# The residual held as upper and lower halves of images: 48 loads of whole images for 160 pieces, one store per piece for two

## The reference, cut to what matters

```python
x = x + conv(_ln_c(x), ...)        # an involution: 7x7 filters that depend on the position
t = to_tokens(x)                   # 16 * 3136 = 50176 tokens of 64 channels
t = t + ffn(_ln_t(t), ...)         # 8 experts, each token goes to its best 2
x = from_tokens(t, x)              # back to images x channels x positions
```

## Time and profile before

| | |
|---|---|
| time, median of 3 runs | 2610.99 us (2604.84 to 2629.76) |
| the profiled execution's own time | 2621.96 us |
| its span, first to last instruction | 2619.3 us |
| mean granted TensorE clock | 0.874 |
| TensorE busy | 2025.6 us (77%) |
| VectorE busy | 1506.3 us (58%) |
| ScalarE busy | 829.4 us (32%) |
| GpSimd busy | 961.0 us (37%) |
| moved by DMA | 474.16 MB, mean 181 GB/s |

### The profile page before, as it was taken

One profiled execution on the slowest core, in us unless ns is written; L12 is line 12 of the kernel. 1 busy time (PEld: TensorE's weight loads), 2 busy tenths in 40 slices (PEclk: granted clock), 3 DMA queues, 4 the chain that ended last, 5 costly groups with the idle time before them and its releaser, 6 DMA issues. The chain is left out here.

```text
span 2619.3 us, 34529 instructions
## 1 busy us (share of the span) xinstructions
PE 2025.6 (77%) x10208; PEld 1223.9 (47%) x10208; DVE 1506.3 (58%) x2687; ACT 829.4 (32%) x1540; POOL 961.0 (37%) x1011
## 2 busy tenths in 40 slices
PE   8959889898898998899898321477778777787855
PEld 5735444454444455445454321345455445454534
DVE  4536666566778777786787535245444444444434
ACT  3421111122222222222222211355445454554520
POOL 6110000004242142331343566155555555555540
PEclk9969999999899999899999555689898898988976
DMA  9877777778776777777773311666667666676539
GB/s 278 176 149 193 184 178 186 196 196 195 181 198 171 203 196 194 182 193 183 195 207 90 89 55 46 174 192 194 187 200 196 194 187 196 195 195 190 164 104 356
DMA packets 284717, 474.16 MB, mean 181 GB/s; under 512 B 116144, under 2 KB 188387, under 8 KB 261565
## 3 DMA queue, kind: packets, MB, share of 16 engines
q1 hardware_dynamic: 247965, 423.23, 60.5%
q0 software_dynamic: 30528, 34.27, 4.8%
q10 hardware_dynamic: 6048, 14.57, 1.5%
HBM read 392.67 MB, written 81.93 MB: 181 GB/s over the span
## 5 line engine op out<-in xcount | busy, mean ns | idle before, releaser
L967 POOL DMA_INDIRECT token_rows<-gate_rows,gate_index x392 | 408.3, 1042 | 1043.4 <-DVE gate_index L1289 930.8
L1167 DVE TENSOR_TENSOR prod<-z_ps,r_all 119x896 f32<-119x896 f32 x512 | 544.8, 1084 | 221.5 <-PE z_ps L1080 110.2
L1500 POOL DMA_INDIRECT mixed<-exp_mix,exp_xt x474 | 491.0, 1036 | 409.8 <-DVE exp_mix L1639 282.7
L1523 ACT ACTIVATE exp_hid<-exp_h_ps,exp_pack 128x384 f32<-128x384 f32 x632 | 349.1, 575 | 419.3 <-PE exp_h_ps L1567 192.8
L1084 PE MATMUL z_ps<-xq,band 112*119 112x448 f32 x1024 | 440.2, 565 | 44.3 <-DVE prod L1167 38.4
L1567 PE MATMUL exp_h_ps<-exp_tok,exp_pack 128*128 128x384 f32 x1264 | 293.0, 377 | 61.7 <-issue 61.2
L1084 PEld LDWEIGHTS z_ps<-xq,band 112*119 112x119 f32 x1024 | 182.1, 187 | 254.8 <-issue 190.7
L1567 PEld LDWEIGHTS exp_h_ps<-exp_tok,exp_pack 128*128 128x128 f32 x1264 | 237.1, 208 | 79.9 <-issue 74.2
L1097 PE MATMUL o_ps<-prod,pick 119*32 119x448 f32 x2048 | 247.9, 578 | 26.9 <-issue 17.2
L1579 PE MATMUL exp_y_ps<-exp_hid,exp_pack 128*64 128x384 f32 x1264 | 262.4, 540 | 1.1 <-issue 1.1
L1078 PE MATMUL z_ps<-xq_hi,band_hi 119*119 119x448 f32 x512 | 215.1, 420 | 51.3 <-DVE xq_lo L1156 21.7
(11 more groups left out here) (205 smaller groups left out, 2161.6 us busy)
## 6 DMA issues: line engine op xcount, KB each, us to landing
xq<-xs SPq DMA_DIRECT2D x192, 896.0 KB
exp_pack<-packs SPq DMA_DIRECT2D x316, 321.5 KB
exp_xt<-token_rows SPq DMA_DIRECT2D x158, 120.0 KB
xs<-xpad SPq DMA_DIRECT2D x32, 448.0 KB, 5.8
xin<-in_x_dram SPq DMA_DIRECT2D x8, 1568.0 KB, 11.0
co<-ob SPq DMA_DIRECT2D x512, 24.5 KB
merge_yt<-mixed ACTq DMA_DIRECT2D x28, 448.0 KB, 6.0
mixed<-exp_mix,exp_xt POOLq DMA_INDIRECT x474
```

The source lines that it names most:

```text
L967: pool.indirect_dma_start(out=token_rows[:, :], out_offset=bass.IndirectOffsetOnAxis(ap=index[b % RR][:, j:j + 1], axis=0), in_=rows[b % R ...
L1167: nc.vector.tensor_tensor(prod[(NU * t + u) % PR][:, :, :].rearrange("p m (d x) -> p m d x", d=D), z_ps[(NU * t + u) % 3][0:MF, :, 0:CN].r ...
L1500: pool.indirect_dma_start(out=mixed[:, :], out_offset=bass.IndirectOffsetOnAxis(ap=xt[t % XT][:, j, ROW_ID:ROW_ID + 1].bitcast(U32), axis= ...
L1523: nc.scalar.activation(hid[n % 8][:, :], h_ps[n % HT][:, 0:N], ACT.Gelu, bias=pack[t % WT][:, e, PACK_B1 + blk:PACK_B1 + blk + 1]).then_in ...
```

## The change: what it does, and the diff

The lanes of `base` now hold another layout. Lanes 0 to 63 hold the upper half of an image (28 rows of positions, HALF = 1568 columns) and lanes 64 to 127 its lower half; the 16 images stand one after the other along the columns, even images first, then odd ones. 16 x 1568 columns are the same 28 x 896 as before.

- `load_base(k)` now takes one whole image, every eighth tile: `x` in a single transfer to all 128 lanes, and `co` in two transfers of 64 lanes. That makes 16 x 3 = 48 transfers in place of 160. CT is 2 instead of 3, with longer buffers.
- `add_conv(n)` runs every fourth tile on half an image's columns (784): 32 additions in place of 28.
- The last pass stores the two halves of the lanes together, with `pieces(d)` of the first 28 chunks. The announced numbers are 42 stores for 84; the built programs have 40 for 80.
- `token_id` is numbered so that step d of the last pass finds chunk d and chunk d + 28 side by side in `mixed`, where before it found chunks 2d and 2d + 1.

```diff
-            pool.iota(tab.token_id[:, :, :].rearrange("p (d u) j -> p d u j", u=2),
-                      pattern=[[2 * CHUNK, CHUNKS // 2], [1, 2], [2, GROUP]], base=0,
+            pool.iota(tab.token_id[:, :, :].rearrange("p (u d) j -> p u d j", u=2),
+                      pattern=[[1, 2], [2 * CHUNK, CHUNKS // 2], [2, GROUP]], base=0,
                       channel_multiplier=2 * GROUP).then_inc(counted, 1)
...
-    CT = 3
-    sum_at = {5 * d + 4: d for d in range(DUAL)}
+    CT = 2
+    HALVES = B * 2
+    sum_at = {4 * n + 6: n for n in range(HALVES)}
...
-            def load_base(d):
-                if d >= CT:
-                    sp.wait_ge(base_done, d - CT + 1)
+            def load_base(k):
+                img = PARITY * (k % (B // PARITY)) + k // (B // PARITY)
+                if k >= CT:
+                    sp.wait_ge(base_done, 2 * (k - CT + 1))
+                sp.dma_start(flat_base[:, HALF * k:HALF * (k + 1)],
+                             x[img].rearrange("c h w -> c (h w)").rearrange("c (h x) -> h c x", h=2)
+                             ).then_inc(base_in, 16)
                 for h in range(2):
-                    lanes = slice(C * h, C * (h + 1))
-                    for img, at, to, size in pieces(2 * d + h):
-                        sp.dma_start(base[lanes, d, to:to + size],
-                                     x[img].rearrange("c h w -> c (h w)")[:, at:at + size]).then_inc(base_in, 16)
-                        sp.dma_start(conv[d % CT][lanes, to:to + size],
-                                     co[img].rearrange("c h w -> c (h w)")[:, at:at + size]
-                                     ).then_inc(conv_in[d % CT], 16)
+                    sp.dma_start(conv[k % CT][C * h:C * (h + 1), :],
+                                 co[img].rearrange("c h w -> c (h w)")[:, HALF * h:HALF * (h + 1)]
+                                 ).then_inc(conv_in[k % CT], 16)
...
-                if t + 2 in sum_at:
-                    load_base(sum_at[t + 2])
+                if t + 3 in sum_at and sum_at[t + 3] % 2 == 0:
+                    load_base(sum_at[t + 3] // 2)
...
-            flat = out.rearrange("b c h w -> b c (h w)")
+            flat = out.rearrange("b c h w -> b c (h w)").rearrange("b c (h x) -> b h c x", h=2)
 
             def store(d):
                 sp.wait_ge(added, d + 1)
-                for h in range(2):
-                    for img, at, to, size in pieces(2 * d + h):
-                        sp.dma_start(flat[img][:, at:at + size],
-                                     res[d % RING][C * h:C * (h + 1), to:to + size]).then_inc(res_out[d % RING], 16)
+                for img, at, to, size in pieces(d):
+                    sp.dma_start(flat[img][:, :, at:at + size],
+                                 res[d % RING][:, to:to + size]
+                                 ).then_inc(res_out[d % RING], 16)
```

More of the change, by code:

```diff
@@ L1397, in expert_stage @@
     BLK = HID // P
-    DUAL = CHUNKS // 2
-    CT = 3
-    sum_at = {5 * d + 4: d for d in range(DUAL)}
+    CT = 2
+    HALVES = B * 2
+    sum_at = {4 * n + 6: n for n in range(HALVES)}
     with ExitStack() as ctx:
@@ L1420, in expert_stage @@
         mix = [sb(f"mix{i}", [P, TILE_BLOCKS, C]) for i in range(3)]
-        conv = [sb(f"conv{i}", [P, CHUNK]) for i in range(CT)]
+        conv = [sb(f"conv{i}", [P, HALF]) for i in range(CT)]
         h_ps = [ps(f"h_ps{i}", [P, 512]) for i in range(HT)]
@@ L1425, in expert_stage @@
         t_ps = ps("t_ps", [P, 512])
+        flat_base = base[:, :, :].rearrange("p d x -> p (d x)")
         spec_in = sem("spec_in")
@@ L1640, in weigh, with add_conv @@
                                         ALU.add).then_inc(mixed_done, 1)
[L1642 to L1647, removed]
+            def add_conv(n):
+                k, part = divmod(n, 2)
+                dve.wait_ge(base_in, (k + 1) * 16)
+                dve.wait_ge(conv_in[k % CT], (k // CT + 1) * 2 * 16)
+                at = HALF // 2 * part
+                now = flat_base[:, HALF // 2 * n:HALF // 2 * (n + 1)]
+                nc.vector.tensor_tensor(now, now, conv[k % CT][:, at:at + HALF // 2], ALU.add).then_inc(base_done, 1)
             for t in range(3):
@@ L1686, in merge_stage @@
         res_out = [sem(f"res_out{i}") for i in range(RING)]
-        runs = [len(pieces(2 * d)) + len(pieces(2 * d + 1)) for d in range(DUAL)]
+        runs = [len(pieces(d)) for d in range(DUAL)]
         block = ctx.enter_context(nc.Block())
```

## The result

The change makes the kernel slower: 3046.1 us median (3033.1 to 3060.0) against 2607.9 us for the kernel before, timed beside it, a ratio of 1.165 with a 95% interval of 1.161 to 1.170. The profiled execution took 3060.0 us (span 3058.1, clock 0.817), 438 us more than the profiled one of before; forecast were 318.

A forecast was written before the change was run, and what follows sets the result against it. It took a circular chain of scatters, rows, weights and TensorE to bound the expert stage, and the DMA engines the last pass. 2622 + 224 (last pass) + 94 (x loads) = 2940, less 11: 2929 us, range 2800 to 3080.

The forecast's parts named there:

- The dealing over engines: New x loads and last-pass stores: 2 x 64 rows against 128 lanes puts each on two DMA engines; forecast given 0.80.
- Part 1, the last pass: Last pass: stores on two engines at 24.7 GB/s make it 298 us instead of 74.3, +224 us.
- Part 2, the gap: Expert stage: behind each x load the next tile's weights land about 20 us late, one gap in eight tiles.
- Part 2, the seven tiles: Expert stage: the other seven of eight tiles speed up from 5.44 to 4.2 us each, as SP gets ahead.
- the sum: Whole kernel: 2622 + 224 for the last pass + 94 for the x loads = 2940, less 11: 2929 us.
- the ceiling that stood in the text: Expert stage: upper bound for the x loads, the seven tiles staying at 5.44 us, +233 us.
- the circle of buffers: Expert stage: landed scatter, rows, weights and TensorE form a chain that holds a tile at 5.44 us.
- Part 3, SP's issues at 0: SP's issues: 160 become 48, 67 us less issue time, worth up to 67 us but counted 0.
- Dealt over sixteen: Rival, chance 0.10, x loads and stores: sixteen engines carry them, nothing waits; 2578 us, faster.
- Two engines, but hidden loads: Rival, chance 0.06, expert stage: catching up is complete, only the last pass pays; 2835 us.
- SP itself stands: Rival, chance 0.04: an issue behind each image load holds SP 10 us, sixteen times, adding 160 us; 3089 us.

The follow-up runs named there:

- e1: The change with x loaded in two transfers of 64 lanes per image, stores as in the change: 2800.6 us, ratio 1.079 to the kernel before.
- e2: The change with each last-pass store in two transfers of 64 lanes, x loaded as in the change: 2836.4 us, ratio 1.091 to the kernel before.
- e5: The change with stores in two 64-lane transfers and each image's x in four, of 57 and 7 lanes per half: 2757.7 us, ratio 1.058.
- e6: The change with stores in two 64-lane transfers and each image's x in four, of 60 and 4 lanes per half: 2618.5 us, ratio 1.001.
- e8: The kernel before with each filter band loaded by two transfers, of 16 x 7 and 7 rows: 2523.6 us, ratio 0.969.
- e7: The change with each tile's three indirect scatters replaced by one plain transfer, sorting back left out: 2859.7 us, one run.
- e10: The change with each tile's three indirect scatters replaced by three plain transfers of 256-byte rows, sorting back left out: 2873.6 us, one run.
- e9: The change with x and stores in 64-lane halves, and each tile's three indirect scatters replaced by one plain transfer, sorting back left out: 2409.9 us, one run.
- e3: The change with both x loads and stores in two transfers of 64 lanes: 2598.7 us, ratio 1.001 to the kernel before.

## Why the prediction was right, and where it was not

- **The dealing over engines** (the forecast, 0.80): right. Two engines for each x load and each store, in the packet records and in e1, e2; the count's arithmetic in e5 and e6; the band itself, from which it was read, in e8 and in its packets. The Trainium skill, "DMA: Bandwidth & Descriptors", section "Why a DMA increments its semaphore by 16 and not by 1", has the rule: the largest count up to 16 that divides the slowest count of both sides. The traces agree with it at 1 (the band), 2 (x loads and stores), 3 (57 lanes) and 16 (64 lanes).
- **Part 1, the last pass:** forecast +224, measured +216. I had taken 24.7 GB/s for each engine, it was 25.6, and the pass took 290.7 us for 298. The gap of SP before the first store was 6.7 us, for 6.
- **Part 2, the gap:** forecast 20 us, measured 20.1 to 25.0 with an average of 22.1, which is 34 us more over sixteen. It ends with the token rows behind the image, not with the weights that I had named.
- **Part 2, the seven tiles: the term that was mis-sized.** I took 4.2 us, "near the floor, with 0.3 for the clock"; they take 5.16, which is 108 us more over sixteen times seven. An eight is 22.1 + 7 x 5.16 = 58.3 us in place of 49.4. From the first gelu of the stage to the last pass it is 1105 us (1662.0 to 2767.45) for 873 (1671.9 to 2545.0), +232, and not the +94 of the sum. It equals the ceiling that stood in the text (+233), but by coincidence: that was reckoned with a shorter gap (20) and slower tiles (5.44). That is the whole error: 138 us too little here, 8 too much in part 1, and a stage that began 10 us earlier in this execution make the 120 us between 438 and 318. My step was: "in the wait SP gets ahead, and the other seven can go faster than today". SP does get ahead: from the issue of a tile's weights to its first matmul the median is 9.4 us, where it was 3.8. In e7 and e10 the tiles then do go at 3.65 us, so the rows and weights are there. What held them at 5.16 are GpSimd's indirect scatters, and the tiles of the new layout without gaps at 5.4 as well (e9 against e3). For the kernel before, which has the same scatters and the same 5.4, this is inferred, not run. I had read the circle of buffers as the cause of the 5.44; it was a thing that fitted, since POOL's own sum (3.9 us a tile) said that it had time to spare. Two views of the kernel before spoke against it. SP's own waits have a single one for a landed scatter in the whole stage:

```profile
SPq L1458 <- DMA mixed<-exp_mix,exp_xt: 1.5, 1, 1.5
```

And the "remote" waits, 182.8 us on ACT's gelu alone, did not fit a circle; they stood in the view of groups by line, and I had not asked what they were.
- **Luck in the range.** The range held because the ceiling took the tiles at today's 5.44, not because the sum had the right reason for their pace. Its upper end had been cut from 3096 to 3080 for a combination called unlikely, and the result came within 34 us of it.
- **Part 3, SP's issues at 0:** right, e3 is 1.001.
- **The rivals.** Dealt over sixteen: falls, as above. Two engines, but hidden loads: falls, the gaps are there. SP itself stands: the x load's issue takes 0.62 us, the weights' behind it 4.30 in the rows shown, and ACT is waiting meanwhile for the rows issued before them. In the last pass it does happen: an issue takes 6.6 us in the median, but there DVE waits for the same stores, and part 1 comes out without a cost of SP's own.

## What to carry to other kernels

Before two transfers are joined into one, look at the outermost count on both sides: what divides both, up to 16, is the number of engines that work on it, and 2 x 64 against 128 leaves 2. Splitting off the remainder cures it, as 16 x 7 + 7 rows for 17 x 7 did. Such a transfer doesn't only take long itself; whatever stands behind it in its queue has a share on the slow engines and lands late too. Look for the same in what is already there: a first transfer of a stage that lands late per byte (11.9 us for 110.6 KB) was worth 3% of this kernel, more than anything the new layout could bring. And a rate that several engines share without one of them being full should be explained by its waits, each kind of them, before it is used as a bound for catching up.

## What the hardware showed that was not expected

- Indirect transfers on GpSimd delay other engines. With 474 of them the tiles take 5.2 to 5.4 us, with 474 plain ones of rows of the same size 3.65 in most and 3.86 on average. That is 172 us (e10), 186 us (e7) and 189 us (e9) of the kernel, while GpSimd idles for 410 us to 656 us of the stage. Which path carries it (the writing of descriptors, or the signals between engines) no run tells.
- An engine's rate depends on how many work beside it. In the change, packets of 6272 bytes took 301 ns on average with up to three of them under way (the image's `x` on two engines) and 416 ns with fourteen or more. In e3, where all the residual's loads lie on sixteen, they took 445 ns. With three slow engines at work alone (e5) it was 355 ns.
- SP's issue of a transfer takes longer where the engines that it goes to have a backlog: 0.608 us in the median for 64-lane stores (e3), 6.6 us for the 128-lane ones.
